# Two chained adapter layers on one core: the 24 identity products at the head of TensorE's queue are left out

## The reference, cut to what matters

```python
# layer 0: a full weight, plus a mixture of 8 low-rank adapters (rank 16), two of them per token
base   = einsum('btd,od->bto', x, W)                     # 1024 x 1024
logits = einsum('btd,ed->bte', x, Wr) + bias(language)   # 8 experts
gates  = softmax of the two largest logits, zero elsewhere
h      = einsum('btd,erd->bter', x, A)
x      = x + base + 2.0 * einsum('bter,bte,eor->bto', h, gates, B)
# layer 1: one 1024 x 1024 weight out of 16 for each of the 8 batch rows
x      = x + einsum('bsi,boi->bso', x, weight[adapter_ids])
```

## Time and profile before

| what | us |
|---|---|
| median of 3 runs (lowest, highest) | 396.96 (396.77, 397.57) |
| the profiled execution | 396.9 |
| its span, first to last instruction | 395.1 |
| TensorE matmuls busy | 389.8 (99%) |
| VectorE busy | 307.9 (78%) |
| ScalarE busy | 173.8 (44%) |

### The profile page before, as it was taken

How to read it: one execution, slowest core, us unless ns; L and a number is a source line. 1 busy time by engine, 2 the same in 40 slices (tenths; PEclk the granted TensorE clock), 3 DMA queues, 4 the chain that set the end, 5 groups by cost and what they waited for, 6 DMA issues and landing times.

```text
span 395.1 us, 5948 instructions
## 1 busy us (share of the span) xinstructions
PE 389.8 (99%) x1888; PEld 329.9 (83%) x1888; DVE 307.9 (78%) x415; ACT 173.8 (44%) x245; POOL 60.7 (15%) x86
## 2 busy tenths in 40 slices
PE   8999999999999999999999999999999999999996
PEld 8888988888889888888888888888888888888886
DVE  3899998988554757048877967999999999999600
ACT  3362283554400243254275334555665656556411
POOL 3134300000000000000110211332321231312000
PEclk9999999999999999999999999999999999999999
DMA  7999750113776100009492999999999999897212
GB/s 202 226 224 216 109 147 2 53 55 107 234 217 165 25 1 0 2 1 247 130 330 71 274 265 273 274 253 278 259 280 291 286 267 302 256 268 166 80 53 55
DMA packets 88129, 68.60 MB, mean 174 GB/s; under 512 B 16386, under 2 KB 87074, under 8 KB 87586
## 3 DMA queue, kind: packets, MB, share of 16 engines
q1 hardware_dynamic: 61472, 46.59, 49.2%
q10 hardware_dynamic: 26626, 21.64, 17.9%
HBM read 53.51 MB, written 14.68 MB: 173 GB/s over the span
## 4 chain that ended last, share of the span: by engine, by line
PE 97%; DMA 1%; SPq 1%; issue 0%; DVE 0%; ACT 0%
PE banks L1421 15%; PE banks L1419 15%; PE banks L1420 15%; PE banks L1282 13%; PE banks L1284 13%; PE banks L1283 13%; PE banks L1275 6%; PE banks L1260 2%; PE banks L1296 2%; PE banks L1293 2%; PE banks L1295 2%; DMA sums<-in_L_cond_Wr_dram 1%; PE banks L1314 0%; SPq L436 0%; SPq L483 0%; SPq L429 0%
## 5 line engine op out<-in xcount | busy, mean ns | idle before, releaser
L1282 PE MATMUL banks<-ring,weights 128*128 128x512 f32 x192 | 75.2, 392 | 0.0
L1420 PE MATMUL banks<-weights,tokens 128*128 128x512 f32 (+1 forms) x184 | 69.9, 380 | 0.0
L1421 PE MATMUL banks<-weights,tokens 128*128 128x512 f32 (+1 forms) x184 | 69.9, 380 | 0.0
L1419 PE MATMUL banks<-weights,tokens 128*128 128x512 f32 (+1 forms) x184 | 69.9, 380 | 0.0
L1106 ACT ACTIVATE weights<-weights_f 128x1024 fp32r<-128x1024 f32 x44 | 46.6, 1061 | 50.1 <-DVE weights_f L759 49.3
L512 POOL TENSOR_TENSOR raw<-raw,ident 128x128 f32<-128x128 f32 x42 | 30.0, 714 | 219.2 <-DMA raw<-in_L_cond_weight_dram 219.1
L759 DVE STREAM_TRANSPOSE weights_f<-raw 128x1024 f32<-128x1024 f32 x42 | 51.7, 1232 | 8.2 <-POOL raw L512 7.7
L765 DVE TENSOR_TENSOR weights<-weights_f,weights 128x1024 fp32r<-128x1024 f32 x44 | 52.7, 1198 | 0.7 <-ACT weights L1106 0.6
L1284 PE MATMUL banks<-ring,turned_w 128*128 128x512 f32 x128 | 49.8, 389 | 0.0
L1283 PE MATMUL banks<-tokens,weights 128*128 128x512 f32 x128 | 49.8, 389 | 0.0
L1282 PEld LDWEIGHTS banks<-ring,weights 128*128 128x128 f32 x192 | 36.0, 188 | 7.6 <-issue 0.3
(11 more groups left out here) (131 smaller groups left out, 626.0 us busy)
## 6 DMA issues: line engine op xcount, KB each, us to landing
raw<-in_L_cond_weight_dram SPq DMA_DIRECT2D x168, 128.0 KB, 5.2
ring_f<-in_L_cond_weight_dram SPq DMA_DIRECT2D x88, 128.0 KB, 5.5
out_dram<-sums ACTq DMA_DIRECT2D x31, 256.0 KB, 5.6
raw<-in_x_dram SPq DMA_DIRECT2D x48, 128.0 KB, 3.3
x_kept<-stage ACTq DMA_DIRECT2D x24, 256.0 KB, 3.1
raw<-in_L_cond_W_dram SPq DMA_DIRECT2D x16, 128.0 KB, 3.4
turned_w_f<-in_x_dram SPq DMA_DIRECT2D x12, 128.0 KB, 3.4
ring_f<-in_L_cond_W_dram SPq DMA_DIRECT2D x12, 128.0 KB, 3.6
```

What stands on the lines that cost most here:

```text
L1282: nc.tensor.matmul(ps, u_hi, x_hi, start=first and k == 0, stop=False, skip_group_check=True)
L1419: nc.tensor.matmul(ps, x_hi, w_hi, start=m == 0, stop=False)
L1420: nc.tensor.matmul(ps, x_hi, w_lo, start=False, stop=False)
L1421: mm = nc.tensor.matmul(ps, x_lo, w_hi, start=False, stop=m == M - 1)
```

## The change

The constant `WARM`, TensorE's first wait and the loop of 24 products go. `first_products()` stays as it was and becomes the first thing on TensorE's queue. Nothing else is edited.

```diff
@@ -29,7 +29,6 @@
     GATE_STEPS = 10
-    WARM = 24
     assert ER == P and M == 8 and T == 2 * P and SPANS == 2 and HALF == HM * P
@@ -1243,10 +1242,6 @@
         @block.tensor
         def _(pe):
-            pe.wait_ge(consts, 3)
-            for _ in range(WARM):
-                nc.tensor.matmul(banks[:, 0, 0:P], ident[:], ident[:], start=True, stop=True)
-
```

## The result

The changed kernel takes 398.48 us (median of 9 runs, 397.86 to 399.85) against 396.96 us: a ratio of 1.0042 with a 95% interval of 1.0031 to 1.0054, so 1.7 us slower, between 1.2 and 2.1 us. The forecast was 399.5 us with a range of 398.2 to 400.5 us. The direction, the mechanism and the range held; the size of 2.6 us was some 1 us too large.

A forecast was written before the change was run, and what follows sets the result against it. TensorE was taken to bound the kernel, its matmuls covering 99% of the span. Products gave 0 us, the low clock in the features lost 2.9 us, taken as 2.6: 396.96 + 2.6 = 399.5 us, range 398.2 to 400.5 us.

The forecast's parts named there:

- The products themselves: Ahead of the features: removing the 24 products' 8.43 us, hidden behind the landing of `Wr`, gives 0 us.
- The durations, not the granted clock of the views, tell the level: Early TensorE passes: spacing of 213 then 112 ns means 1.2 GHz until about 7.6 us, though views grant 1.00.
- The delay of 5.9 us: TensorE's first work runs at the low level for 5.9 us; moved into the features, this loses 2.9 us.
- I cost this at nothing in either direction: After the features: no notable TensorE waits, so lateness is not given back; recovered 0 to 0.1 us.
- Elapsed time: Rival: the clock rises at 7.6 us by time since program start, so time stays 396.96 us; chance 0.08.
- The longer low level: Rival: low level lasts past the features into the first product, some 405 to 410 us; chance 0.07.
- The gain ahead of the features: Rival: without identity reads `fac` is ready at most 0.35 us earlier; shares a 0.03 remainder with a short delay.
- The bound of 0.35 us on an earlier `fac`: Before the features: VectorE waited only 0.34 us for `Wr` after turning `A`, so `fac` gains at most 0.35 us.

The follow-up runs named there:

- e12: Kernel before with 12 identity products instead of 24, profiled a second time; that execution took 400.61 us.
- e1: Kernel before with 4 identity products instead of 24: median 398.12 us, ratio 1.0026.
- e7: Changed kernel (no products) with the loads of `Wr` issued ahead of those of `A`: 399.20 us, ratio 1.0048 to the kernel before.
- e3: Kernel before with 20 identity products instead of 24: median 396.93 us, ratio 1.0005.
- e4: Kernel before with 40 identity products instead of 24: median 399.33 us, ratio 1.0053.
- e5: Kernel before with 12 products instead of 24, started only once VectorE has turned the first half token tile: 397.51 us, ratio 1.0005.
- e6: Kernel before, 24 products kept, with the loads of `Wr` issued ahead of those of `A`: 397.39 us, ratio 1.0011.
- e2: Kernel before with 12 identity products instead of 24, first profile: median 398.11 us, ratio 1.0036; the profiled execution was the fastest, 397.06 us.
- e9: Kernel before, unchanged, profiled a second time: 397.26 us.
- e10: Kernel before, unchanged, profiled a third time: 396.97 us.

## Why the prediction was right, and its size too large

*The products themselves are free.* Right: TensorE's first instruction is at 10.81 us, it follows `fac` as before.

*The durations, not the granted clock of the views, tell the level.* Right, and the clock record bears it out with its first entry at 7.60 us. The features' first weight loads took 335 ns, a pass 232 ns (forecast 332 and 227 ns), and in e12 the view shows 0.50 under just such passes.

*The delay of 5.9 us.* The reading was at the high end. From the first pass of a run of work to the rise the clock record has 5.9, 4.7 and 5.1 us for the kernel before, 5.6, 5.3 and 3.5 us for the changed one, 3.5 us (e1), 3.7 us (e7), 3.2 and, after the fall, 5.1 us (e12), 5.4, 4.3, 4.9 and 5.6 us (e3, e4, e5, e6), and 6.2 us (e2, where the last 0.7 us of it are idle). The length of the products or features tells the same without that record: for the second and third execution of the kernel before the 48 identity passes took 7.87 and 8.06 us instead of 8.43 us, and each us of delay less takes 0.47 us off them. The feature groups that began at the low level were 1.7 to 2.7 us longer, 2.3 us on average over the three profiles of the changed kernel and 2.2 us over all six, where the sum had 2.9 us and the forecast took 2.6 us. The page "TensorE: Matmul & The Clock Gate" of the Trainium skill, in Part 1, has about 4 us and half a microsecond of scatter between runs; these readings have 3.2 to 6.2 us, so they vary by more. By its figure the loss would be 2.0 us, an estimate (4 × 0.49) under the 2.3 us measured.

*"I cost this at nothing in either direction."* This term was mis-sized too, by some 0.5 us. The prediction ruled out a recovery because the one profile showed no wait of TensorE behind 10.55 us. That profile was of an execution in which `fac` was late. In e9 and e10 TensorE reaches product 2 ahead of VectorE, so the first 0.6 or 0.7 us of lateness are free there. Over the whole program, time less end of the features is 382.38 us in the first profile of the kernel before, 383.24 and 383.14 us in e9 and e10, and 382.36 us on average in the three profiles of the changed kernel: 0.56 us on average that lateness does not cost. With the features' extra 2.34 us and 0.04 us that they start later on average (10.19 against 10.15 us), the sum over three profiles each is 2.34 + 0.04 − 0.56 = 1.8 us, which is what these six executions differ by. The runs have 1.7 us by the ratio and 1.5 us by the medians. That this split holds over all runs is inferred from the few profiled executions, not shown for the others.

*The rivals.* Elapsed time is out: the first rise stands anywhere from 4.91 us (e12) to 16.39 us (changed kernel). What e2 adds is that the level can also rise 0.7 us after the work has stopped. The longer low level did not come: in all six executions whose features began at the low level the rise lies within them. The gain ahead of the features did not show: `fac` was ready at 10.77, 9.90 and 9.79 us without products and at 10.50, 10.01 and 9.82 us with them, 0.04 us apart on average with a scatter of up to a microsecond; an effect of some tenths could hide in it and stays open. The bound of 0.35 us on an earlier `fac` was read from one execution and does not hold across them: in e9 `fac` was 0.5 us earlier with the products in place, since `Wr` landed earlier and VectorE was done with `A` earlier.

## What to carry to other kernels

Products that compute nothing can be worth their place: what they buy is read from the spacing of the same instruction early and late in the trace, and it counts if they lead up to the first real work: with 1.1 us between nothing was lost, while of two profiled executions with twelve early products one kept the high level to the features and one had lost it 2.1 us after the last product. Before a wait is costed at nothing because the trace does not show it, ask how much earlier the engine would have to arrive to meet it: in one profile no wait showed, in two others TensorE was ahead by 0.6 and 0.7 us. And a size that hangs on one event of one execution deserves a second profile, or a range that starts well below it.

## What the runs showed of the hardware

The level of TensorE's clock changes while the engine is idle, both ways: it rose 0.7 us after the last of twelve products (first profile, at 7.90 us) and it fell 2.1 us after the last of them (second profile, at 8.3 us), with the same kernel. In the kernel with 20 products an idle time of 1.1 us lost nothing. From the start of sustained work to the rise it took 3.2 to 6.2 us over 14 executions. The landing of `Wr`, counted from the issue of its last load, took 4.2 to 5.6 us from execution to execution under otherwise equal queues (4.24 us in e1, 5.58 us in the first profile after): a scatter of 1.3 us in the start of TensorE's work, nearly what the change costs.
